# A two-layer vision tower on one core: value moves waited for part by part, attention pairs finished two at a time, and other idle products

## The chip, the core and the metric

The kernel runs on one NeuronCore of a Trainium2 chip, as one launch. The metric is the device time in microseconds, and lower is better. The core has TensorE (matmuls, written to the accumulation memory PSUM), VectorE, ScalarE, GpSimd, and SyncE, whose queue here only starts DMA transfers. Each engine works through its own list of instructions in order and waits on semaphores for the others.

## The reference

The input is 16 images of 3x96x96. They become 36 patches each and a class token, so 37 tokens of width 256 per image and 592 in all, which the kernel holds in five tiles of 128 rows. Then, with residual additions:

```python
h = tokens(x)                                   # patch embedding, class token, positions
h = h + attention0(layernorm(h))                # 16 heads of 16, quantised, ternary weights
h = h + ffn0(layernorm(h))                      # shared expert and the best two of 8 experts
h = h + tower1(layernorm(h))                    # two attention layers (global, local), 4 value heads
w = (weights >= 0.0) * 2.0 - 1.0                # last projection
h = h + clip(layernorm(h) @ w.T * scale + bias, -100, 100)
```

The end of the first attention matters most here:

```python
att = jnp.einsum('bhnr,bhmr->bhnm', ql, kl) / math.sqrt(dk)
y = jax.nn.softmax(att, axis=-1) @ v
y = y.transpose(0, 2, 1, 3).reshape(B, N, d)
return quant4(y) @ ternary_weight(Wo_w).T
```

`quant4` takes the largest absolute value of each token's row, divides by it, multiplies by 7 and rounds.

## The kernel before

Nothing schedules the work. The order on each engine is the order in which the code for that engine is written, and every dependence is a semaphore written by hand. An operation that writes "waits y" runs when the semaphore `y` has reached a count.

**The pair loop of the first tower.** The 16 images are taken as 8 pairs. For a pair, TensorE does `probs_T` (transposes the probabilities of pair p, L1561), `scores` of pair p + 2 (L1549), `values` of pair p (L1574) and four idle products (`spare_products`, L1593); in the last two pairs four wider idle products (`spare`, L1436) stand in the place of the scores. Idle products compute nothing that is read. They give TensorE work between its tasks. `spare` and `spare_products` multiply bf16 data, and `keep_clock` (L1442) multiplies 128x512 fp32 data, which the trace shows as two records each. VectorE does `shift(p)` (row maxima, L895, and their subtraction, L901) and then `finish_y(p - 2)`: the reciprocal of the softmax sums (L911), the product with it (L913), the row maximum for the quantisation (L918), its scaling (L919), its reciprocal (L921) and the rounding (L922). ScalarE does the exponentials (L534), copies the transposed probabilities out of PSUM (L540), and converts the rounded rows (L544, `whole_y`). `values` of pair p writes PSUM bank 6 + p % 2, so it waits until the pair before the last has been read (semaphore `y`):

```python
for p in range(PAIRS + 2):
    if p < PAIRS:
        shift(p)
    if p >= 2:
        finish_y(p - 2)
```

After the loop, TensorE turns the rows (`turn_y`, L1610), spreads the factors of the quantisation over the tokens (L1620, waits `ma7`), does one `keep_clock` product, and then the attention's output product (L1630, waits `yT`).

**The second tower, twice.** `project(t)` computes queries, keys and, from tile 2 on, values of token tile t (L1860). ScalarE copies these values into `v_tok` (L664). The attention needs them per image in `vo`, and since images don't begin at a tile's border, SyncE moves them with small DMAs (L465): 20 per layer, for images 8 to 15, in group 2 (images 8 to 11) and group 3 (12 to 15). TensorE's `values(grp)` (L1931) waits for the moves of its group, `d_v2` or `d_v3`. Images 0 to 7 take another way, without DMAs.

**The last projection.** TensorE writes the bias into the banks of the first four tiles (`bias(t)`, L1972, a product with one row of ones; each waits until VectorE has read that bank, semaphore `bn`), transposes the normalised rows (L1643, waits `xn`), and multiplies in three products per half of the contraction (L1662 to L1664). VectorE clips (L1315), adds (L1316), and SyncE stores.

The functions that the diff touches:

## Time and profile before

| what | value |
|---|---|
| median of 3 runs | 330.63 us (328.04 to 330.92) |
| the profiled execution, its own time | 332.31 us |
| its span, first to last instruction | 330.3 us |
| busy share of the span: TensorE, VectorE, ScalarE, GpSimd | 94%, 66%, 49%, 46% |
| TensorE's mean granted clock | 0.967 of full |

The span leaves out the start and the end of the launch, 2.0 us here. The busy share of TensorE counts idle products too, so 94% says little about how much of it is needed. The chain of waits, followed back from the last instruction, says more.

### The profile page before, as it was taken

The page shows a single profiled execution, that of the slowest core. Times are in us where ns is not written, and L with a number is a line of the kernel's source. Part 1 is how long each engine was busy: PE and PEld are TensorE (multiplying, and loading weights), DVE is VectorE, ACT ScalarE, POOL GpSimd, SP SyncE. Part 2 cuts the span into 40 slices and gives each one's busy share as a digit, 9 for nine tenths or more (in the row PEclk, how much of TensorE's full clock was granted, in tenths as well). Part 3 has the DMA queues.
Part 4 walks back from the last instruction along what each step waited for, and adds up shares of the span by engine and source line. Part 5 has one row for each costly group of instructions (what it writes and reads, how often), then busy time and mean ns, then how long its engine had stood idle before and what let it go on. Part 6 is the DMA issues. An engine that isn't in the chain of part 4 may idle for free.

```text
span 330.3 us, 8349 instructions
## 1 busy us (share of the span) xinstructions
PE 309.3 (94%) x3406; PEld 260.3 (79%) x3408; DVE 217.0 (66%) x574; ACT 160.4 (49%) x353; POOL 153.1 (46%) x178
## 2 busy tenths in 40 slices
PE   7999999999898898999999999999699998999886
PEld 5775678876588888999999999999575676567765
DVE  1089898997877434455655545453577986898674
ACT  0304575556343135576667676763221694169410
POOL 1201209910334782698879888986582000410020
PEclk9999999998979979999999999999979999999987
DMA  7992001320021252537666566514800000000002
GB/s 267 403 396 92 3 0 57 127 99 2 1 96 50 89 167 83 177 127 240 212 221 203 183 217 206 196 34 119 269 4 0 3 9 5 2 1 9 5 2 73
DMA packets 18879, 36.74 MB, mean 111 GB/s; under 512 B 4602, under 2 KB 12849, under 8 KB 18840
## 3 DMA queue, kind: packets, MB, share of 16 engines
q1 hardware_dynamic: 17440, 33.35, 30.2%
q0 software_dynamic: 960, 2.43, 2.3%
q8 instruction: 28, 0.46, 0.5%
q10 hardware_dynamic: 440, 0.41, 0.5%
q14 instruction: 11, 0.09, 0.1%
HBM read 30.28 MB, written 5.75 MB: 109 GB/s over the span
## 4 chain that ended last, share of the span: by engine, by line
PE 60%; DVE 17%; SPq 8%; issue 5%; ACT 5%; DMA 2%; another core or an unknown queue 1%; POOL 1%; ACTq 0%; DVEq 0%; POOLq 0%
PE ps L1662 13%; PE ps L1663 11%; PE ps L1664 11%; SPq L465 8%; PE ps L1442 4%; PE ps L1860 3%; PE ps L1549 2%; PE ps L1454 2%; PE ps L1449 1%; DMA vo<-v_tok 1%; PE ps L1517 1%; PE ps L1561 1%; DVE stats L789 1%; PE ps L1824 1%; PE ps L1574 1%
## 5 line engine op out<-in xcount | busy, mean ns | idle before, releaser
L1339 POOL TENSOR_TENSOR w0l<-raw,w0h 128x384 fp32r<-128x384 f32 (+1 forms) x60 | 56.3, 975 | 15.7 <-ACT w0h L573 15.3
L1089 DVE TENSOR_TENSOR ps<-gact,ps 128x256 f32<-128x256 f32 (+3 forms) x60 | 26.2, 437 | 40.6 <-ACT gact L592 39.0
L1355 POOL TENSOR_TENSOR rstd<-vtmp,cst 128x3 f32<-128x3 f32 (+1 forms) x8 | 6.7, 840 | 91.3 <-DVE vtmp L799 46.3
L1339 POOL TENSOR_TENSOR w1l<-raw,w1h 128x384 fp32r<-128x384 f32 (+1 forms) x48 | 44.8, 971 | 6.5 <-ACT w1h L573 5.7
L592 ACT ACTIVATE gact<-ps 128x256 f32<-128x256 f32 (+3 forms) x60 | 23.2, 387 | 24.8 <-PE ps L1664 16.5
L1094 DVE TENSOR_TENSOR hrl<-ps,hrh 128x256 fp32r<-128x256 f32 (+1 forms) x48 | 20.3, 423 | 18.5 <-ACT hrh L596 17.6
L596 ACT ACTIVATE hrh<-ps 128x256 fp32r<-128x256 f32 (+1 forms) x48 | 18.5, 384 | 27.2 <-DVE ps L1089 26.0
L1662 PE MATMUL ps<-xg0h,w1h 128*128 128x256 f32 x88 | 25.8, 293 | 0.0
L1662 PE MATMUL ps<-xg1h,w0h 128*128 128x256 f32 x88 | 25.6, 291 | 0.0
L1442 PE MATMUL ps<-cst 128*128 128x512 f32 x54 | 25.3, 614 | 0.0
L1663 PE MATMUL ps<-xg1l,w0h 128*128 128x256 f32 x88 | 24.9, 283 | 0.0
L1663 PE MATMUL ps<-xg0l,w1h 128*128 128x256 f32 x88 | 24.9, 283 | 0.0
L1664 PE MATMUL ps<-xg1h,w0l 128*128 128x256 f32 x88 | 24.9, 283 | 0.0
L1664 PE MATMUL ps<-xg0h,w1l 128*128 128x256 f32 x88 | 24.9, 282 | 0.0
L1442 PEld LDWEIGHTS ps<-cst 128*128 128x128 f32 x54 | 10.1, 194 | 10.4 <-issue 10.0
L573 ACT ACTIVATE w0h<-raw 128x768 fp32r<-128x768 f32 (+1 forms) x24 | 18.0, 800 | 0.0
L573 ACT ACTIVATE w1h<-raw 128x768 fp32r<-128x768 f32 (+1 forms) x24 | 17.8, 800 | 0.0
L1662 PEld LDWEIGHTS ps<-xg1h,w0h 128*128 128x128 f32 x88 | 16.8, 191 | 0.5
L1662 PEld LDWEIGHTS ps<-xg0h,w1h 128*128 128x128 f32 x88 | 16.8, 191 | 0.5
L1662 PE MATMUL ps<-w0h,hrh 128*128 128x256 f32 (+1 forms) x48 | 14.0, 293 | 3.3 <-DVE hrl L1094 3.1
L1663 PEld LDWEIGHTS ps<-xg1l,w0h 128*128 128x128 f32 x88 | 16.9, 192 | 0.0
L1664 PEld LDWEIGHTS ps<-xg1h,w0l 128*128 128x128 f32 x88 | 16.9, 191 | 0.0
(309 smaller groups left out, 898.7 us busy)
## 6 DMA issues: line engine op xcount, KB each, us to landing
raw<-in_wexp SPq DMA_DIRECT2D x18, 768.0 KB, 4.3
raw<-in_wexp SPq DMA_DIRECT2D x9, 640.0 KB, 4.4
xg_d<-zero SPq DMA_DIRECT2D x8, 256.0 KB, 10.7
xgs<-xg_d SPq DMA_DIRECT2D x8, 256.0 KB, 4.6
stage_l<-in_xT SPq DMA_DIRECT2D x6, 320.0 KB, 5.0
yg_d<-y SPq DMA_DIRECT2D x7, 256.0 KB
stage_l<-in_tokW SPq DMA_DIRECT2D x6, 128.0 KB, 5.0
stage_l<-in_wq SPq DMA_DIRECT2D x1, 512.0 KB, 5.2
```

Source lines behind the costliest of these rows:

```text
L465: sp.dma_start(vo[n0:n0 + m, b, :, e, :], src[:, :, e, :]).then_inc(S(f"d_v{grp}"), 16)
L573: A(wset[x % 2][0][:, o:o + n], raw[:, o:o + n], ACT.Copy).then_inc(S("w_hi"), 1)
L592: A(gact[i % 2][rows_of(c), 0:n], gate[:, 0:n], ACT.Silu).then_inc(S("silu"), 1)
L596: A(dst[rows_of(c)], product, ACT.Copy).then_inc(S("hh"), 1)
L1089: V.tensor_tensor(up, gact[i % 2][rows_of(c), 0:n], up, ALU.mult).then_inc(S("hm"), 1)
L1094: V.tensor_tensor(dst[r], product, hi[r].bitcast(F32), ALU.subtract).then_inc(S("hl"), 1)
L1339: last = nc.gpsimd.tensor_tensor(wset[i][1][w], raw[w], wset[i][0][w].bitcast(F32), ALU.subtract)
L1442: M(bank(b), ones, cst[:, 0:BK], start=True, stop=True)
L1662: M(dst, a[0], b[0], start=start, stop=False, skip_group_check=skip)
L1663: M(dst, a[0], b[1], start=False, stop=False, skip_group_check=skip)
L1664: return M(dst, a[1], b[0], start=False, stop=stop, skip_group_check=skip)
L1860: last = M(bank(QKB[t % 2])[:, 0:width], xnT[:, k, t * P:(t + 1) * P], w["wq"][:, k, 0:width], start=(k == 0), stop=(k == DC - 1))
```

## The change

It has three parts.

1. SyncE's wait for `v_tok` stands before each piece of an image's rows, and asks only for the tile in which the piece lies. Before, it stood once per group and asked for the last tile of the group. The moves and their order are the same.
2. In the first tower `finish` takes two pairs at a time for pairs 0 to 5, with instructions of twice the size, behind both shifts of the next two pairs. Pairs 6 and 7 are finished singly. `spare_products` has two products instead of four. Behind the pair loop, two bf16 idle products stand ahead of the wait for the factors, and three bf16 ones stand where one `keep_clock` product stood.
3. At the last projection two `keep_clock` products stand between the third bias and the transposes, and three bf16 idle products behind the transposes. The fourth bias comes behind them.

```diff
+        FINISH = [(p, 2) for p in range(0, PAIRS - 2, 2)] + [(PAIRS - 2, 1), (PAIRS - 1, 1)]
...
             for li in range(2):
                 for grp in (2, 3):
-                    sp.wait_ge(S("v_tok"), (TT - MOVED) * li + grp + 2 - MOVED)
-                    if li == 0:
+                    if li == 0 and grp == 2:
                         sp.wait_ge(S("cleared"), 2)
                     for b in range(4 * grp, 4 * grp + 4):
                         for lo, hi in rows_of_batch(b):
+                            sp.wait_ge(S("v_tok"), (TT - MOVED) * li + lo // P + 1 - MOVED)
                             for e in range(2):
...
-            def finish_y(p):
-
-                dve.wait_ge(S("y_mm"), p + 1)
-                yv = bank(6 + p % 2)[:, 0:H * VW].rearrange("p (j w) -> p j w", w=VW)
-                link(V.reciprocal(rz[:, p % 2, :], yv[:, :, DH]))
-                y = yq[:, p, :]
-                V.tensor_tensor(y.rearrange("p (j w) -> p j w", w=DH), yv[:, :, 0:DH],
-                                rz[:, p % 2, :].unsqueeze(2).to_broadcast([P, H, DH]),
-                                ALU.mult).then_inc(S("y"), 1)
-                dve.wait_ge(S("y"), p + 1)
-                m = ma2[:, p:p + 1]
+            def finish(first, n):
+
+                done = FINISH.index((first, n)) + 1
+                pairs = slice(first, first + n)
+                dve.wait_ge(S("y_mm"), first + n)
+                yv = bank(6 + first % 2, n).rearrange("p (a c) -> p a c", a=n)[:, :, 0:H * VW].rearrange(
+                    "p a (j w) -> p a j w", w=VW)
+                z = rz[:, first % 2:first % 2 + n, :]
+                link(V.reciprocal(z, yv[:, :, :, DH]))
+                y = yq[:, pairs, :]
+                V.tensor_tensor(y.rearrange("p a (j w) -> p a j w", w=DH), yv[:, :, :, 0:DH],
+                                z.unsqueeze(3).to_broadcast([P, n, H, DH]), ALU.mult).then_inc(S("y"), 1)
+                dve.wait_ge(S("y"), done)
+                m = ma2[:, pairs]
                 link(V.tensor_reduce(m, y, AX_X, ALU.max, apply_absolute_value=True))
                 V.tensor_scalar(m, m, 1e-6, 1.0 / 7.0, ALU.max, ALU.mult).then_inc(S("ma7"), 1)
-                dve.wait_ge(S("ma7"), p + 1)
-                link(V.reciprocal(rma[:, p:p + 1], m))
-                V.tensor_scalar(y, y, rma[:, p:p + 1], MAGIC, ALU.mult, ALU.add).then_inc(S("yr"), 1)
-
-            for p in range(PAIRS + 2):
-                if p < PAIRS:
-                    shift(p)
-                if p >= 2:
-                    finish_y(p - 2)
+                dve.wait_ge(S("ma7"), done)
+                link(V.reciprocal(rma[:, pairs], m))
+                for p in range(first, first + n):
+                    V.tensor_scalar(yq[:, p, :], yq[:, p, :], rma[:, p:p + 1], MAGIC, ALU.mult,
+                                    ALU.add).then_inc(S("yr"), 1)
+
+            for i in range(PAIRS // 2):
+                shift(2 * i)
+                shift(2 * i + 1)
+                if i >= 1:
+                    finish(2 * i - 2, 2)
+            finish(PAIRS - 2, 1)
+            finish(PAIRS - 1, 1)
...
                 pe.wait_ge(S("pt"), p + 1)
                 if p >= 2:
-                    pe.wait_ge(S("y"), p - 1)
+                    pe.wait_ge(S("y"), p // 2)
...
             def spare_products():
-                for _ in range(4):
+                for _ in range(2):
...
             for p in range(PAIRS - 1):
                 turn_y(p)
-            pe.wait_ge(S("ma7"), PAIRS)
+            spare(2, 5)
+            pe.wait_ge(S("ma7"), len(FINISH))
...
             turn_y(PAIRS - 1)
-            keep_clock(1, 1)
+            spare(3, 5)
...
-            for t in range(4):
+            for t in range(3):
                 pe.wait_ge(S("bn"), TT * 4 + t + 1)
                 bias(t)
+            pe.wait_ge(S("bn"), TT * 4 + 4)
+            keep_clock(2, 3)
             transposes(4)
+            spare(3, 3)
+            bias(3)
```

How the instructions stand in a row, at three places. The line numbers of the changed kernel are a few higher.

SyncE in layer 0, the moves of group 2 (`vo` is where the values go, `v_tok` where they come from). Before:

```order
L465 DMA vo<-v_tok 37x2x16 [waits cleared,v_tok]
L465 DMA vo<-v_tok 37x2x16 x3
L465 DMA vo<-v_tok 14x2x16 x2
L465 DMA vo<-v_tok 23x2x16 x2
L465 DMA vo<-v_tok 37x2x16 x2
```

The same ten moves in the changed kernel:

```order
L466 DMA vo<-v_tok 37x2x16 [waits v_tok,cleared]
L466 DMA vo<-v_tok 37x2x16
L466 DMA vo<-v_tok 37x2x16 [waits v_tok]
L466 DMA vo<-v_tok 37x2x16
L466 DMA vo<-v_tok 14x2x16 [waits v_tok]
L466 DMA vo<-v_tok 14x2x16
L466 DMA vo<-v_tok 23x2x16 [waits v_tok]
L466 DMA vo<-v_tok 23x2x16
L466 DMA vo<-v_tok 37x2x16 [waits v_tok]
L466 DMA vo<-v_tok 37x2x16
```

No move changes its place. The six up to the 14 rows of image 10 lie in tile 2 and wait for its copy alone, and the other four wait for tile 3.

VectorE in the first tower (`mx` are row maxima, `rz` reciprocals of sums, `ma` the factors of the quantisation). Before, from the shift of pair 2 on:

```order
L895 TENSOR_REDUCE mx<-ps 128x8 [waits sc_mm]
L895 TENSOR_REDUCE mx<-ps 128x8
L901 TENSOR_TENSOR stage_l<-ps,mx 128x296 [waits pt_mm,dve_chain]
L901 TENSOR_TENSOR stage_l<-ps,mx 128x296
L911 RECIPROCAL rz<-ps 128x16 [waits y_mm]
L913 TENSOR_TENSOR stage_l<-ps,rz 128x256 [waits dve_chain]
L918 TENSOR_REDUCE ma<-stage_l 128x1 [waits y]
L919 TENSOR_SCALAR ma<-ma 128x1 [waits dve_chain]
L921 RECIPROCAL rma<-ma 128x1 [waits ma7]
L922 TENSOR_SCALAR stage_l<-stage_l,rma 128x256 [waits dve_chain]
```

In the changed kernel, from the shift of pair 3 on:

```order
L896 TENSOR_REDUCE mx<-ps 128x8 [waits sc_mm]
L896 TENSOR_REDUCE mx<-ps 128x8
L902 TENSOR_TENSOR stage_l<-ps,mx 128x296 [waits pt_mm,dve_chain]
L902 TENSOR_TENSOR stage_l<-ps,mx 128x296
L916 RECIPROCAL rz<-ps 128x32 [waits y_mm]
L918 TENSOR_TENSOR stage_l<-ps,rz 128x512 [waits dve_chain]
L922 TENSOR_REDUCE ma<-stage_l 128x2 [waits y]
L923 TENSOR_SCALAR ma<-ma 128x2 [waits dve_chain]
L925 RECIPROCAL rma<-ma 128x2 [waits ma7]
L927 TENSOR_SCALAR stage_l<-stage_l,rma 128x256 [waits dve_chain]
L927 TENSOR_SCALAR stage_l<-stage_l,rma 128x256
```

The finish of pair 0 has moved behind the shift of pair 3 and takes pair 1 with it: seven instructions for two pairs where twelve stood.

TensorE at the last projection (`sml` holds the bias, `cst` constants, `xn` the normalised rows). Before:

```order
L1972 MATMUL ps<-sml,cst 128x256 [waits bn] x4
L1643 MATMUL ps<-cst,xn 128x128 [waits xn]
L1643 MATMUL ps<-cst,xn 128x128
...
L1643 MATMUL ps<-cst,xn 128x128 [waits xn]
L1643 MATMUL ps<-cst,xn 128x128
```

In the changed kernel:

```order
L1981 MATMUL ps<-sml,cst 128x256 [waits bn] x3
L1450 MATMUL ps<-cst 128x512 [waits bn]
L1450 MATMUL ps<-cst 128x512
...
L1652 MATMUL ps<-cst,xn 128x128 [waits xn]
L1652 MATMUL ps<-cst,xn 128x128
L1444 MATMUL ps<-sq,identb 128x512 x3
L1981 MATMUL ps<-sml,cst 128x256
```

Two wide idle products stand ahead of the transposes and three behind them, and the fourth bias is now the last thing before the projection's products.

## Rows read from the trace of the kernel before

**Rows 1.** The page, chain of waits by engine, shares of the span

```profile
PE 60%; DVE 17%; SPq 8%; issue 5%; ACT 5%; DMA 2%; another core or an unknown queue 1%; POOL 1%; ACTq 0%; DVEq 0%; POOLq 0%
```

**Rows 2.** Timeline of VectorE in the pair loop: start us, us, engine, line, operation, idle before

```profile
53.62 0.84 DVE L895 TENSOR_REDUCE mx<-ps 128x8 f32<-128x296 f32 x2 [1.37 <-PE ps L1549]
...
66.73 0.25 DVE L911 RECIPROCAL rz<-ps 128x16 f32<-128x16 f32 x1
67.01 0.42 DVE L913 TENSOR_TENSOR stage_l<-ps,rz 128x256 f32<-128x256 f32 x1
...
68.31 0.35 DVE L922 TENSOR_SCALAR stage_l<-stage_l,rma 128x256 f32<-128x256 f32 x1
68.58 0.83 DVE L895 TENSOR_REDUCE mx<-ps 128x8 f32<-128x296 f32 x2
...
70.20 0.25 DVE L911 RECIPROCAL rz<-ps 128x16 f32<-128x16 f32 x1
```

**Rows 3.** Groups by line, 52 to 80 us: busy us, mean ns, idle before

```profile
L922 DVE TENSOR_SCALAR stage_l<-stage_l,rma 128x256 f32<-128x256 f32 x8 | 3.9, 486 | 0.3
```

**Rows 4.** Timeline of VectorE, rotation in layer 0 of the second tower

```profile
255.58 0.82 DVE L1218 TENSOR_TENSOR stage_l1a<-ps,rot_s 128x640 f32<-128x640 f32 x1 [1.07 <-PE ps L1860]
```

**Rows 5.** Timeline of TensorE, one pair of the pair loop

```profile
54.27 0.61 PE L1593 MATMUL ps<-sq,identb 128*128 128x256 bf16 x4
54.72 0.82 PE L1561 MATMUL ps<-cst,stage_l 128*111 128x128 f32 x6
...
57.50 0.61 PE L1593 MATMUL ps<-sq,identb 128*128 128x256 bf16 x4
```

**Rows 6.** Chain of waits ahead of the attention output: start us, us, what

```profile
78.78 1.28 PE ps L1620 x10
...
80.20 1.82 PE ps L1442 x2
```

**Rows 7.** Stretches: us, busy per engine (x instructions), granted clock, DMA share, GB/s

```profile
80.00:81.00 1.00, 1.00 (x5) 0.44 (x4) 0.83 (x3) 0.82 (x2) 0.00 (x0) 0.53 0.00 0
83.00:84.00 1.00, 1.00 (x9) 1.00 (x8) 0.96 (x3) 1.00 (x2) 0.00 (x0) 0.76 0.00 0
319.00:320.00 1.00, 0.49 (x2) 0.09 (x2) 0.94 (x2) 0.89 (x4) 0.00 (x0) 0.50 0.00 0
```

**Rows 8.** Timeline of ScalarE, values of token tile 2, layers 0 and 1

```profile
259.14 0.22 ACT L664 ACTIVATE v_tok<-ps 128x64 f32<-128x64 f32 x1 [1.16 <-PE ps L1860]
...
292.30 0.23 ACT L664 ACTIVATE v_tok<-ps 128x64 f32<-128x64 f32 x1 [0.70 <-PE ps L1860]
```

**Rows 9.** Timeline of SyncE's queue, the moves of both layers

```profile
261.23 14.47 SPq L465 DMA_DIRECT2D vo<-v_tok  x20
...
294.52 14.13 SPq L465 DMA_DIRECT2D vo<-v_tok  x20
```

**Rows 10.** Timeline of TensorE, first record of the last values product, both layers

```profile
277.26 0.34 PE L1931 MATMUL ps<-stage_l1b,vo 128*32 128x74 f32 x8 [1.44 <-DMA vo<-v_tok]
...
310.17 0.34 PE L1931 MATMUL ps<-stage_l1b,vo 128*32 128x74 f32 x8 [1.05 <-DMA vo<-v_tok]
```

**Rows 11.** Timeline of TensorE: idle products, bias, transposes, last projection

```profile
245.49 7.13 PE L1442 MATMUL ps<-cst 128*128 128x512 f32 x16
...
314.99 1.99 PE L1972 MATMUL ps<-sml,cst 1*128 1x256 f32 x8
317.42 2.07 PE L1643 MATMUL ps<-cst,xn 128*128 128x128 f32 x10 [0.44 <-DVE xn L807]
320.23 0.55 PE L1662 MATMUL ps<-wfh,xTh 128*128 128x256 f32 x1 [0.74 <-DVE xTl L1311]
```

**Rows 12.** Groups by line, 314 to 330 us, the clips of the last projection

```profile
L1315 DVE TENSOR_SCALAR xn<-ps 128x256 f32<-128x256 f32 x5 | 2.1, 424 | 3.1 <-PE ps L1664 3.1
```

**Rows 13.** Chain of waits in the last projection

```profile
321.00 0.21 PE ps L1664
...
326.83 0.12 PE ps L1664
```

## The prediction

> **What bounds the kernel now.** I read the chain of waits first. TensorE holds 60% of it, VectorE 17%, and SyncE's queue 8%, although SyncE computes nothing [rows 1]. That is the sign that instructions which only start transfers stand on the path. Then I took the three places that the change touches, each with the timeline of the engines that meet there, and asked which wait ends last.
>
> In the pair loop of the first tower, VectorE waits once, 1.37 us before pair 2's first reduction at 53.62, and from there has work without a gap until the factors of pair 7 are ready, just before TensorE uses them at 78.78 [rows 2, 6]. One pair costs it a shift (68.58 to 70.20, 1.62) and a finish (66.73 to 68.58, 1.85), so 3.47 us [rows 2]. TensorE needs 3.23 us for a pair (54.27 to 57.50), 0.45 of them idle products (54.27 to 54.72) [rows 5]. So TensorE leads at first and VectorE is the bound by the end.
>
> In the second tower both layers look alike. SyncE starts 20 small moves of values, one after the other, in 14.47 and 14.13 us [rows 9], and TensorE stands still 1.44 and 1.05 us before the last values product, waiting for them to land [rows 10].
>
> At the last projection TensorE had 0.50 of its clock from about 319 on, the 1.2 GHz level [rows 7]. What it had done before that was eight records of one-row bias products, a pause of 0.44 us, ten transposes and a pause of 0.74 us [rows 11]. At that level a product of 128x256 takes 0.21 us, at 2.4 GHz 0.12 [rows 13], so six for a tile take 1.28 against VectorE's 0.88, and VectorE stands idle 3.1 us in all before its five clips [rows 12].
>
> **The pair loop.** A finish is now done for two pairs at once. What does an instruction of twice the size cost? The rotation over 640 elements took 0.82 us and the product over 256 took 0.42 [rows 2, 4], so 384 elements more cost 0.40, and 256 more 0.27. Of the six steps of a finish, the product and the reduction grow by 0.27 each, the small ones by 0.03 together, and a second rounding costs 0.27 (68.31 to 68.58). So 1.85 becomes about 2.70 for two pairs instead of 3.70. That is 1.00 saved three times, 3.0 us; pairs 6 and 7 stay single.
>
> Against it stands the new order. Pair 0 is finished only behind the shift of pair 3, so VectorE waits for the scores of pair 3, one TensorE period behind those of pair 2. With half the idle products that period is 3.23 - 0.23 = 3.00, so pair 3's shift begins at about 56.5 and the wait is some 1.4 us. From there VectorE has five shifts (8.1), three double finishes (8.1), one single (1.85) and the last up to its factors (1.35): 56.5 + 19.4 = 75.9, and I add 0.3 for short waits on TensorE, which now needs as long for two pairs (6.0) as VectorE (5.94). That is 76.2 against 78.73 before, a gain of 2.5.
>
> One correction. The eight roundings took 0.486 on average where an undisturbed one took 0.35 [rows 2, 3], 1.1 us over in all, the early ones, when GpSimd splits weights. The double finish of pairs 0 and 1 still falls into that time with two roundings back to back. I take 0.5 off, between 0 and 1.3: **2.0 us gained**, from 0.9 to 2.6. The Trainium skill, "SBUF — State Buffer", section "SBUF: two separate sides", calls this an exclusive lock: a VectorE operation in a two-port mode and a GpSimd operation shut each other out for the whole instruction. By it both roundings could be held and the term would be 1.2; no row shows two in a row, so my value stays.
>
> Half the idle products save TensorE 0.23 a pair, which is hidden wherever VectorE is the later one; it is in the 3.00 above and is not counted again. The new wait of the values product is for the double finish that frees two banks. For pair 2 this is ready at about 59.2, when TensorE arrives at 59.4; for pair 6 it is late by some 0.2 (in the 0.3). ScalarE's conversion of pair 0 to whole numbers waits behind the same finish and holds the next copy of probabilities, which TensorE needs only behind the scores of the pair after next.
>
> **Ahead of the attention output.** One full-precision idle product took 1.82 us there, on the path, at a granted clock of 0.53 [rows 6, 7], against 0.89 at full clock (sixteen records in 7.13) [rows 11]. Three small ones of 512 columns cost 3 x 0.22 at full clock and 3 x 0.43 = 1.3 at half. So **0.5 us gained**, from 0 (its data are late) to 0.9 (the clock stays up). The two new ones ahead of the factors fit into VectorE's last finish.
>
> **The second tower.** The first six moves read the token tile whose values are ready 1.84 us sooner in layer 0 (259.14 + 0.22 against a start at 261.23) and 2.0 us in layer 1 (292.30 + 0.23 against 294.52) [rows 8, 9]. They fill some 4 us, and the next tile is there by then, so the whole queue starts and ends that much sooner. What is late next? TensorE had nothing between its own work and the last move for 1.44 and 1.05 us [rows 10]; behind those it is bound by itself. VectorE and ScalarE wait for that product. So **2.5 us gained**. Eight more instructions per layer carry a wait. Layer 0, whose two waits are for two semaphores each, took 0.34 longer than layer 1, so a wait costs at most 0.17, eight at most 1.4. The moves have 0.4 and 0.9 to spare, so the gain could fall to 1.0. A wait of one semaphore adds nothing that layer 1 shows, and I take 2.5.
>
> **The last projection.** Two full-precision idle products (four records, 1.77 at full clock [rows 11]) start behind the third bias product at about 316.2 and end at 318.0. The transposes then run back to back and the first three tiles are through 0.1 later than before. Three small products (0.65) and one bias product fall into the former pause of 0.74. If the clock stays at 2.4 GHz, VectorE waits some 0.6 before its first clip and not again: 3.1 - 0.6 = 2.5, less 0.1. That is **2.4 us for the profiled execution**. If the clock falls anyway the gain is 0, and if it has fallen before, the two products take 3.6 and the loss is up to 2.3.
>
> **Sum.** Against the profiled execution (332.31, span 330.3) it is 2.0 + 0.5 + 2.5 + 2.4 = 7.4, giving 324.9. The median of the runs shown is 330.63, 1.68 less. Part of that may be a shorter stretch at half clock at the end, so for the median I count 1.7 for the last term instead of 2.4: 330.63 - 6.7 = **323.9 us**, 2.0% faster.
>
> **Rivals.**
> The clock is not held at the last projection. For it: transposes were the last things before both falls shown [rows 6, 7, 11]. Against it: 1.77 us of dense products are now between. Last term from 0 to +2.3, so 325.6 to 327.9, about 326.2. Chance 15%.
>
> The clock falls once or twice in the pair loop, where only half of the idle products remain. For it: it fell at 80 behind the same kind of small work. Against it: TensorE has no pause there and 0.23 of each 3.00 us is a small share to lose. While it is low TensorE's pair takes up to twice 3.0, so a fall as long as the one from 80 to 83.5 costs 1.7 [rows 7]. Two give 327.3. Chance 12%. The Trainium skill, "TensorE: Matmul & The Clock Gate", section "Part 4: PE-mode transpose", says that transposes don't count as busy for the clock in the way that products do. By it this rival gains weight, and so does the one above; that transposes stand just before the falls at 80 and 319 agrees with it [rows 6, 11].
>
> Instructions of twice the size cost twice the time. Then a double finish saves nothing, the wait for pair 3 stays, and the factors come at 79.7, 1.0 later than before: 323.9 + 3.0 = 326.9. The 640-element row speaks against it [rows 4]. Chance 8%.
>
> The added waits cost 0.17 each, which takes 1.5: 325.4. Chance 5%.
>
> **Slower:** the clock stays low through the whole pair loop. Each pair then costs TensorE up to 6.0 in place of 3.0 and seven pairs lose 21 us: 345. It would need four such pairs to turn 6.7 us of gain into a loss over 1%. The low stretch at 80 ended after 3.5 us of dense work, and that is the ground against it. Chance 4%.
>
> **How the numbers follow.** The forecast holds 56%. The range runs from 321.5 (all upper bounds together give 322.2, and the median is one of three runs that lie 2.9 apart) to 327.5, which takes in the first, third and fourth rival and most of the second. Some 1% is what a measurement of this kernel can tell from no change; the runs shown lie 0.9% apart. Under 327.3 lie the forecast and most of the first four rivals, 84%; between 327.3 and 333.9 the rest of them, 12%; above, 4%.
>
> **What would show it.** In the changed kernel: a VectorE wait of some 1.4 us before pair 3's reduction and the factors of pair 7 ready at about 76.2; a double finish of 2.7; both `vo` queues starting right behind the first `v_tok` copy and under 0.2 us of TensorE idle before the last values product; a granted clock of 1.00 in the last ten us and 0.6 us of VectorE idle before its clips. The prediction is wrong if the clock column drops between 52 and 76, if the double finish takes over 3.3, or if the clips still wait for 3 us.

## The result, and the profile after

Over 20 executions each, on one chip, the kernel before took 333.84 us in the median (328.04 to 336.85) and the changed kernel 327.50 (323.89 to 333.28). The ratio is **0.989, 95% interval 0.985 to 0.994**: 1.1% faster, 3.6 us. It compares only the executions within 1.5% of the fastest of the same kernel, 5 of the 20 before and 14 of the 20 after, so it is not the quotient of the medians, which lie 6.3 us apart. The forecast was 6.7 us, 2.0%. The profiled execution took 326.40 us (span 324.4) against 332.31 (330.3), 5.9 less. Its first 1.0 us is no part of the change: pair 2's first reduction begins at 52.60 instead of 53.62 [rows 2], and nothing ahead of it was touched.

The page of the changed kernel, its chain of waits by engine, answers to [rows 1]:

```profile
span 324.4 us, 8319 instructions
...
PE 65%; DVE 20%; ACT 5%; issue 4%; another core or an unknown queue 2%; DMA 1%; POOL 1%; ACTq 0%; DVEq 0%; POOLq 0%
```

SyncE's queue (8% before) has left the chain, and VectorE has 20% of it instead of 17%.

I cut every execution into the same five stages. **A**, pair loop: from pair 2's first reduction to TensorE's product with the factors. **B**: from there to the first addition to `h`. **C**: from layer 0's first rotation on VectorE to layer 1's. **D**: from that to the first bias of the last projection. **E**: from that bias to the last addition. Each is the difference of two start times in the timelines. Before: 25.16, 4.13, 33.08, 26.33, 12.81. After: 24.11, 3.45, 31.97, 25.69, 10.98. That is 1.05 + 0.68 + 1.11 + 0.64 + 1.83 = 5.3 us. What lies between B and C, the experts, is not changed and gave 0.4 back (172.67 to 173.09).

**The pair loop.** Timeline of VectorE in the changed kernel, the first double finish from pair 3's reduction on, the scaling of the second, the end of the third and the two single ones (start, us, what, idle before):

```profile
55.62 0.84 DVE L896 TENSOR_REDUCE mx<-ps 128x8 f32<-128x296 f32 x2 [1.31 <-PE ps L1557]
...
57.25 0.35 DVE L916 RECIPROCAL rz<-ps 128x32 f32<-128x32 f32 x1
57.63 0.69 DVE L918 TENSOR_TENSOR stage_l<-ps,rz 128x512 f32<-128x512 f32 x1
58.35 0.69 DVE L922 TENSOR_REDUCE ma<-stage_l 128x2 f32<-128x512 f32 x1
59.08 0.49 DVE L923 TENSOR_SCALAR ma<-ma 128x2 f32<-128x2 f32 x1
...
59.80 0.86 DVE L927 TENSOR_SCALAR stage_l<-stage_l,rma 128x256 f32<-128x256 f32 x2
60.59 0.82 DVE L896 TENSOR_REDUCE mx<-ps 128x8 f32<-128x296 f32 x2
...
65.65 0.60 DVE L923 TENSOR_SCALAR ma<-ma 128x2 f32<-128x2 f32 x1
...
72.12 0.17 DVE L923 TENSOR_SCALAR ma<-ma 128x2 f32<-128x2 f32 x1
...
73.05 0.25 DVE L916 RECIPROCAL rz<-ps 128x16 f32<-128x16 f32 x1
...
75.30 0.26 DVE L916 RECIPROCAL rz<-ps 128x16 f32<-128x16 f32 x1 [0.31 <-PE ps L1582]
```

GpSimd in the same stretch (its groups hold several instructions each):

```profile
59.04 2.00 POOL L1381 CAST w0h<-raw 128x384 fp32r<-128x384 f32 x4
...
64.94 1.29 POOL L1386 TENSOR_TENSOR wo0l<-wo0q,wo0h 128x512 fp32r<-128x512 f32 x1
```

VectorE waits 1.31 us for pair 3's scores, as forecast (1.4). The double finish without disturbance, the third, takes 70.29 to 73.05, 2.76 us, as forecast (2.70). The first took 3.34 (57.25 to 60.59) and the second 3.20. Look at the scaling, two elements per partition: 0.17 us in the third, 0.49 and 0.60 in the others. The first began at 59.08, just behind the start of a GpSimd cast at 59.04 (four in 2.00 us, so about 0.5 each), and ended with it. The second began at 65.65 while GpSimd's subtraction of 64.94 ran, and ended at 66.25 where that ended, at 66.23. The clock stayed at 1.00.

**The second tower.** TensorE in layer 0, the end of the values product of group 2 (`values(2)`), the output product behind it, and the last values product; then the one interrupted record of layer 1:

```profile
271.99 0.65 PE L1940 MATMUL ps<-stage_l1b,vo 128*32 128x74 f32 x7
272.40 0.31 PE L1940 MATMUL ps<-stage_l1b,zo 128*32 128x74 f32 x3
272.48 0.23 PE L1940 MATMUL ps<-stage_l1b,vo 128*32 128x74 f32 x1
272.49 0.35 PE L1940 MATMUL ps<-stage_l1b,zo 128*32 128x74 f32 x5
272.77 1.13 PE L1950 MATMUL ps<-wo_g,ozp 128*128 128x256 f32 x4
273.83 0.34 PE L1940 MATMUL ps<-stage_l1b,vo 128*32 128x74 f32 x8
```

```profile
304.17 0.22 PE L1940 MATMUL ps<-stage_l1b,vo 128*32 128x74 f32 x1 [0.20 <-issue]
```

The idle 1.44 and 1.05 us before the last values product [rows 10] are gone. But the product ahead of it, whose 64 multiplications took 1.16 us before (273.54 to 274.70), now took 1.57 (271.20 to 272.77) and in layer 1 1.64. Nothing it waits for is late: the one idle time that the trace names there is "issue", TensorE without instructions.

**The last projection.** TensorE, then VectorE:

```profile
310.91 1.56 PE L1981 MATMUL ps<-sml,cst 1*128 1x256 f32 x6
312.39 1.98 PE L1450 MATMUL ps<-cst 128*128 128x512 f32 x4
314.22 1.25 PE L1652 MATMUL ps<-cst,xn 128*128 128x128 f32 x10
...
316.76 0.35 PE L1671 MATMUL ps<-wfh,xTh 128*128 128x256 f32 x1
```

```profile
315.59 1.68 DVE L1319 TENSOR_TENSOR xTl<-ps,xTh 128x384 fp32r<-128x384 f32 x4 [0.85 <-ACT xTh L737]
317.75 0.42 DVE L1323 TENSOR_SCALAR xn<-ps 128x256 f32<-128x256 f32 x1 [0.47 <-PE ps L1673]
...
321.43 0.42 DVE L1323 TENSOR_SCALAR xn<-ps 128x256 f32<-128x256 f32 x1 [0.42 <-PE ps L1673]
```

```profile
317.00:322.00 5.00, 4.39 (x32) 3.72 (x31) 3.94 (x11) 0.00 (x0) 0.00 (x0) 1.00 0.25 85
```

The granted clock is 1.00 until the last addition is through, and six products for a tile take 0.79 us or less (clips begin at 317.75, 318.55, 319.34). VectorE waits 0.85 + 0.47 + 0.42 = 1.7 us from the last normalised rows on: before the subtraction that needs the transposed rows, before the first clip, and before the last. In the kernel before it was 0.24 for the transposed rows and 3.1 at the clips [rows 12].

### The profile page after: what moved, and what is told of

It is laid out like the page before. It is cut to its first block, busy times and chain, and to the rows that moved or that the text cites. A ratio compares the mean times of both kernels' runs of the same rounds, so it can differ in the third digit from the quotient of the medians.

```text
span 324.4 us, 8319 instructions
## 1 busy us (share of the span) xinstructions
PE 305.1 (94%) x3398; PEld 255.8 (79%) x3402; DVE 216.0 (67%) x559; ACT 160.2 (49%) x353; POOL 153.2 (47%) x178
## 4 chain that ended last, share of the span: by engine, by line
PE 65%; DVE 20%; ACT 5%; issue 4%; another core or an unknown queue 2%; DMA 1%; POOL 1%; ACTq 0%; DVEq 0%; POOLq 0%
PE ps L1671 12%; PE ps L1673 11%; PE ps L1672 10%; PE ps L1869 4%; PE ps L1940 3%; PE ps L1912 3%; PE ps L1557 2%; PE ps L1462 2%; PE ps L1950 2%; PE ps L1450 2%; DVE ps L1097 2%; PE ps L1457 1%; PE ps L1894 1%; PE ps L1569 1%
```

## The experiments

All numbers are of stages as cut above. "Ratio" is against the kernel before on the same chip.

```
kernel                        A      B      C      D      E     ratio (95%)
before                      25.16   4.13  33.08  26.33  12.81   1
changed                     24.11   3.45  31.97  25.69  10.98   0.989 (0.985 to 0.994)
e1_moves                    25.24   3.46  31.81  25.21  12.74   0.998 (0.993 to 1.003)
e2_pairs                    23.91   3.45  33.04  26.32  13.01   0.995 (0.991 to 0.999)
e3_last                     25.14   3.93  33.04  26.32  10.99   0.989 (0.983 to 0.995)
e4_idle_only                27.14   3.46  33.03  26.33  11.64   1.003 (0.998 to 1.007)
e5_pad                      25.17   3.45  31.81  25.20  10.99   0.981 (0.975 to 0.987)
e6_other_form               24.62   3.46  31.98  25.68  10.92   0.985 (0.979 to 0.990)
e7_late_split               23.00   3.45  32.25  25.72  10.99   1.015 (1.010 to 1.020)
e8_one_idle                 27.33   3.46  32.95  25.41  10.70   0.985 (0.980 to 0.989)
e9_short_pool               24.13   3.46  33.31  25.40  10.98   0.982 (0.973 to 0.991)
e10_four_idle               24.41   3.45  31.64  25.63  10.99   0.987 (0.982 to 0.992)
e11_late_weights            24.12   3.45  31.98  25.99  10.99   0.994 (0.989 to 0.999)
e12_together                24.78   3.45  31.72  25.21  10.69   0.987 (0.982 to 0.993)
e13_changed_again           24.10   3.45  32.95  25.41  10.99   0.990 (0.985 to 0.995)
e14_parts_1_and_3           25.22   3.45  31.58  25.21  10.98   0.985 (0.979 to 0.991)
```

A stage is good to some 0.1 us where nothing disturbs it, a ratio to no better than 0.5%. Stages come from one profile of each run. The causes below rest on stages and rows; ratios are only used for the whole. Between B and C lie the experts, which the three parts don't touch and which took 167.1 to 174.1 us (187.8 in e7); that spread is larger than the gain, and it is in every total.

### One part at a time

**e1_moves**: the kernel before with part 1 alone.

```diff
-                    sp.wait_ge(S("v_tok"), (TT - MOVED) * li + grp + 2 - MOVED)
...
+                            sp.wait_ge(S("v_tok"), (TT - MOVED) * li + lo // P + 1 - MOVED)
```

> The kernel before with part 1 alone (a wait ahead of each piece of the value moves). In the changed kernel the idle time of 1.44 and 1.05 us before the last values products is gone, but the values product of group 2 took 1.57 and 1.64 us instead of 1.16, so only 1.10 and 0.65 us came out. Theory 1: these 0.4 us in each layer are pauses in which TensorE waits for its own instructions, and they depend on where in its program the products lie. TensorE's list is here that of the kernel before, so the pauses are absent, the gain is 2.3 to 2.5 us, ratio 0.993. Theory 2: the 0.4 us come from the moves being earlier (their packets or their semaphore events meet the products of group 2). Then they are here too and the gain is 1.75 us, ratio 0.995. In both, no idle time over 0.2 us before the last values products.

Theory 1 holds for the gain: C and D are 1.27 and 1.12 us shorter, 2.4 in all. The values product of group 2 took 1.41 us in layer 0 (271.13 to 272.54) and 1.17 in layer 1, so a pause of 0.25 us is left in layer 0 where none was expected. In e3_last, with the moves as before, it took 1.44 there. The output product that follows and the last values product stand back to back with it.

```profile
271.13 0.34 PE L1931 MATMUL ps<-stage_l1b,vo 128*32 128x74 f32 x8
...
272.30 0.31 PE L1931 MATMUL ps<-stage_l1b,zo 128*32 128x74 f32 x8
272.54 1.13 PE L1941 MATMUL ps<-wo_g,ozp 128*128 128x256 f32 x4
273.60 0.34 PE L1931 MATMUL ps<-stage_l1b,vo 128*32 128x74 f32 x8
```

So part 1 by itself gives what was forecast, and the pauses of 0.4 us and more are not of its making. The ratio, 0.998, doesn't show it: its interval reaches from 0.993.

**e2_pairs**: the kernel before with part 2 alone, its diff as in the change above (`finish`, `spare_products`, and the idle products behind the loop).

> The kernel before with part 2 alone (first tower: two pairs finished at a time, half the idle products, small ones behind the loop). By the trace of the changed kernel: from pair 2's first reduction to TensorE's use of the factors 24.1 us instead of 25.2, from there to the first addition to h 3.45 instead of 4.13, together 1.7 us and a ratio of 0.995. Theory 1 (what VectorE does is the bound, and it is held by GpSimd as before): 24.1 here too, double finishes of 3.3, 3.2 and 2.8 us. Rival: the gain is given back behind the attention, where the clock falls at some other place (granted clock under 0.9 between 78 and 94 us for longer than in the kernel before): ratio 0.998 to 1.002. If the pauses in the second tower hang on where TensorE's program lies, the values products of group 2 take 1.6 us here as in the changed kernel, although the moves are as before.

The loop gains 1.25 us, and the pauses in the values product are here, with the moves as they were: TensorE pauses for some 0.4 us in it, and the idle time before the last values product shrinks by about as much, from 1.44 and 1.05 to 0.98 and 0.55. C and D stay as before.

```profile
272.23 0.66 PE L1940 MATMUL ps<-stage_l1b,vo 128*32 128x74 f32 x7
...
273.02 1.13 PE L1950 MATMUL ps<-wo_g,ozp 128*128 128x256 f32 x4
275.13 0.34 PE L1940 MATMUL ps<-stage_l1b,vo 128*32 128x74 f32 x8 [0.98 <-DMA vo<-v_tok]
```

In the kernel with part 2 alone the pause costs nothing, because it is taken out of a wait. Part 1 removes that wait, and the pause comes to light. The ratio, 0.995, is the one expected for a gain of 1.7 us; its interval leaves room for the rival's 0.998 too. Of these 1.7, 0.68 lie in stage B, and e1 has the same B (3.46) with the old code.

**e3_last**: the kernel before with part 3 alone.

```diff
-            for t in range(4):
+            for t in range(3):
...
+            pe.wait_ge(S("bn"), TT * 4 + 4)
+            keep_clock(2, 3)
             transposes(4)
+            spare(3, 3)
+            bias(3)
```

> The kernel before with part 3 alone (idle products at the last projection). By the trace of the changed kernel, from the first bias to the end of the span 13.5 us instead of 15.3, so 1.8 us and a ratio of 0.9945; VectorE idle some 1.7 us in all from the last normalised rows to its last clip (3.3 before). Rival: in the repeats of the kernel before the clock is often up at this place by itself, and the idle products only delay the transposes there by 0.8 us: a ratio of 0.997 to 1.001 although the profile shows the clock held.

E is 10.99 against 12.81: 1.8 us, and the clock at 1.00. The rival's 0.997 to 1.001 lies outside the interval. The ratio (0.989) is lower than this stage explains (0.9945); its profile began 4 us earlier than the others (pair 2's first reduction at 48.83), which has nothing to do with the edit. The kernel before doesn't always lose the same here: e1 12.74, e2 13.01, and e4, with the same code at this place, 11.64, because the low stretch began at 320.2 there and was half as long.

**e4_idle_only**: the kernel before with the idle products of part 2 alone, pairs finished one by one.

```diff
             def spare_products():
-                for _ in range(4):
+                for _ in range(2):
...
-            keep_clock(1, 1)
+            spare(3, 5)
```

> The kernel before with the idle products of part 2 alone: two instead of four per pair, two and three small ones behind the loop in place of the full-precision one. Pairs are finished one by one as before. Theory 1 (VectorE sets the end of the pair loop, 3.47 us a pair): the factors are used 25.0 to 25.2 us after pair 2's first reduction, as before, and 0.7 us are gained from there to the first addition to h, ratio 0.998. Rival (TensorE sets it): 0.23 a pair less, factors 1 us earlier, ratio 0.995, and finishing two pairs at once would have brought nothing.

Neither theory: the loop took 27.14, 2.0 us more than before. TensorE stood 1.62 us at 68.9 without instructions, and from 71.0 to 74.4 its granted clock was 0.50. That was the rival I had given 12%, with a pause ahead of the fall that I had not foreseen. Because of it this run doesn't tell the two theories apart.

### Where TensorE's instructions lie

**e5_pad**: the changed kernel with 13 small idle products more in a wait of TensorE.

```diff
             keep_clock(3, 0)
+            for _ in range(13):
+                M(bank(0)[:, 0:8], identb[:, :], sq0[:, 0, 0:8], start=True, stop=True)
             transposes(1)
```

> The changed kernel with 13 more idle products of 8 columns on TensorE, ahead of the first transposes behind the attention, where TensorE waits 1.3 us for VectorE anyway. They bring TensorE's list in the second tower back to where it stood in the kernel before, since part 2 took 13 more products out than it put in. Theory 1 (the 0.4 us pauses in the values product of group 2 hang on where TensorE's instructions lie): that product takes 1.16 us again instead of 1.57 and 1.64, the second tower gives 2.4 us instead of 1.75, and the whole is 0.6 us under the changed kernel. Theory 2 (the pauses come from the moves being earlier, or from anything else of the change): 1.6 us as in the changed kernel. The pad itself costs at most 13 x 0.02 us beside the wait.

Theory 1. C and D are 31.81 and 25.20, those of e1 to 0.01 us, 0.65 better than the changed kernel, and the values product of group 2 took 1.41 and 1.16 us as in e1, not 1.16 in both layers. The same stages in the seven profiles with the changed kernel's list of TensorE at this place (changed, e6, e7, e8, e9, e11, e13) add up to between 57.66 and 58.71, 58.10 on average; in the four with the list of before (e1, e5, e12, e14) to between 56.79 and 57.02. With the moves as before it was 59.41. So **the place of the list decides over about half of what part 1 gives**, 1.3 or 2.5 us on average. The same list doesn't give the same pauses each time: in e13, the changed kernel once more, the values products of groups 1 and 2 of layer 0 took 1.55 and 2.15 us, and C was 32.95, hardly less than before. What makes the difference between two executions stays open. Its loop took 25.17, with a fall of the clock from 66.4 to 69.8.

**e11_late_weights**: the changed kernel with the third weight transfer of the pair loop held back.

```diff
             for part in range(3):
+                if part == 2:
+                    sp.wait_ge(S("y_mm"), PAIRS - 1)
                 next_load(1, part)
```

> The changed kernel with the third weight transfer of the pair loop (768 KB, started at about 65 us) held back until the values of pair 6 are through, at about 73 us. In two profiles TensorE's next block of 16 KB of instructions began to land at 68.3 instead of 66.2 while that transfer ran, TensorE stood 1.6 and 1.9 us and the clock fell behind it. Theory 1 (the block waits behind the transfer): it lands from about 66.2 in under 1.0 us instead of 1.3 to 1.6, no pause of TensorE at 69 us (0.25 in the changed kernel), no fall in the loop, 23.9 us for it. Theory 2 (the pauses have another source): 0.2 us or more at the same instruction. ScalarE needs these weights only behind the attention, so nothing should be lost there.

This run is best read beside e8_one_idle (below), the changed kernel up to its last projection, whose loop took 27.33. Timeline of TensorE in e8, and the clock behind it:

```profile
68.55 0.29 PE L1582 MATMUL ps<-stage_l 111*37 111x51 f32 x4
70.73 1.15 PE L1582 MATMUL ps<-stage_l 111*37 111x51 f32 x20 [1.89 <-issue]
```

```profile
66.00:70.70 4.70, 2.84 (x89) 2.39 (x84) 4.09 (x12) 2.42 (x4) 0.02 (x1) 1.00 0.45 156
70.80:74.20 3.40, 3.40 (x30) 2.70 (x30) 2.10 (x6) 0.46 (x1) 0.00 (x0) 0.50 0.02 5
```

The queues in e8 from 66 to 68.3, and then from 68.3 to 70.6 (queue, kind: packets, MB, share of 16 engines; "instruction" brings the engines' instructions in blocks of 16 KB):

```profile
q1 hardware_dynamic: 118, 0.70, 86.2%
```

```profile
q8 instruction: 1, 0.02, 2.7%
```

The same 66 to 68.3 in the changed kernel and in e11:

```profile
q1 hardware_dynamic: 106, 0.65, 84.9%
q8 instruction: 1, 0.02, 4.2%
```

```profile
q8 instruction: 1, 0.02, 2.9%
```

In e8 the block of instructions came only when the weights (86% of the DMA engines) were through, and TensorE stood 1.89 us. In the changed kernel it got in between and TensorE stood 0.25. With the weights out of the way, in e11, it took 1.08 us instead of 1.56, there was no pause at this instruction, and no fall. Theory 1 for this instruction, but the loop stayed at 24.12 instead of the 23.9 expected. VectorE's wait before pair 7's finish did shrink, from 0.31 to 0.11 us. But TensorE paused 0.30 us at another place, among the scores at 65.59, and VectorE's shift behind them came 0.2 later, at 69.34. (e2, with neither pause, took 23.91.) The ratio of e11, 0.994, shows no gain either. That the long pause of e4 and e8 is the wait behind the weights is read from the order of their packets; of the eight profiles with two idle products per pair and the transfer in its place (all such but e7 and e11) six had no long pause, so one profile without it doesn't show that the edit prevents it. In e4 and e8 the fall stands right behind the pause. In e5 it came without one, 2.3 us behind a wait of 0.41 us for ScalarE that the changed kernel has too (0.39), without a fall. What decides there stays open.

### VectorE and GpSimd

**e6_other_form**: the changed kernel with the rounding and the scaling in the three-operand form.

```diff
-                V.tensor_scalar(m, m, 1e-6, 1.0 / 7.0, ALU.max, ALU.mult).then_inc(S("ma7"), 1)
+                V.scalar_tensor_tensor(m, m, 1e-6, seventh[:, 0:n], ALU.max, ALU.mult).then_inc(S("ma7"), 1)
...
-                    V.tensor_scalar(yq[:, p, :], yq[:, p, :], rma[:, p:p + 1], MAGIC, ALU.mult,
-                                    ALU.add).then_inc(S("yr"), 1)
+                    V.scalar_tensor_tensor(yq[:, p, :], yq[:, p, :], rma[:, p:p + 1],
+                                           cst[:, C_UNM:C_UNM + 1].to_broadcast([P, D]), ALU.mult,
+                                           ALU.subtract).then_inc(S("yr"), 1)
```

> The changed kernel with the rounding and the scaling of the row maxima written in VectorE's three-operand form (scalar_tensor_tensor, the constant read from a tile) instead of tensor_scalar. Theory 1: the tensor_scalar form is held while a GpSimd instruction runs (the scaling took 0.49 and 0.60 us instead of 0.17, and ended with GpSimd's cast and subtraction), and the three-operand form, like the product with the reciprocals (0.69 us in all three double finishes), isn't. Then the scaling takes some 0.2 us everywhere, the rounding about 0.45 everywhere instead of 0.31 undisturbed, the three double finishes cost about 3.0 each instead of 3.34, 3.20 and 2.76, and the loop is within 0.4 us of the changed kernel. Theory 2: the holding hits any VectorE instruction that reads and writes SBUF only: 0.5 to 0.6 for the scaling and over 0.8 for the first two roundings again, and the loop is 0.8 us longer.

```profile
59.45 0.52 DVE L925 SCALAR_TENSOR_TENSOR ma<-ma,seventh 128x2 f32<-128x2 f32 x1
...
66.31 0.59 DVE L925 SCALAR_TENSOR_TENSOR ma<-ma,seventh 128x2 f32<-128x2 f32 x1
...
73.00 0.16 DVE L925 SCALAR_TENSOR_TENSOR ma<-ma,seventh 128x2 f32<-128x2 f32 x1
```

Theory 2 on what is held: 0.52 and 0.59 against 0.16 undisturbed. The form doesn't help, and the rounding costs 0.13 more each time; the loop is 0.5 us longer, not 0.8. As a rule for every instruction between SBUF and SBUF theory 2 is too wide: the reduction ahead of the scaling took 0.69 in all three double finishes, although in the changed kernel the one of 64.92 ran beside GpSimd's subtraction of 64.94. The Trainium skill, "SBUF — State Buffer", section "SBUF: two separate sides", counts a VectorE instruction with two inputs in SBUF among those that contend with a reading GpSimd instruction; by that rule this form had to be held, and the trace agrees. The product with the reciprocals, one of whose inputs lies in PSUM, took 0.69 in all three double finishes.

**e7_late_split**: the changed kernel with GpSimd's weight split behind the loop.

```diff
+                    pool.wait_ge(S("ma7"), len(FINISH))
                     for part in range(3):
                         pool.wait_ge(S(f"d_raw{part}"), 16)
```

> The changed kernel with GpSimd's casts and subtractions for the weights of the first expert (11.6 us of work) put behind the factors of the last pair; the subtraction for the attention's output weights, 1.3 us, stands ahead of them. GpSimd is idle in the pair loop, and the weight transfers that wait for its buffers come later too. Theory 1 (VectorE was held by GpSimd for about 1.0 us in all): all three double finishes take 2.76 us, and the factors are used 23.1 us after pair 2's first reduction instead of 24.1. Rival (TensorE's periods and its instruction pauses are as near a bound as VectorE): double finishes of 2.76 us but the loop not under 23.8, with VectorE waiting for TensorE instead. Behind the loop some of the gain, or more, can be lost at the first expert, whose weights are late.

```profile
58.90 0.17 DVE L923 TENSOR_SCALAR ma<-ma 128x2 f32<-128x2 f32 x1
...
59.30 0.61 DVE L927 TENSOR_SCALAR stage_l<-stage_l,rma 128x256 f32<-128x256 f32 x2
59.83 0.83 DVE L896 TENSOR_REDUCE mx<-ps 128x8 f32<-128x296 f32 x2
```

Theory 1, to 0.1 us: all three double finishes take 2.76, the loop 23.00. So GpSimd costs the changed loop 1.1 us, not 0.5. (The weight transfers left the loop with it, but 1.0 of the 1.1 is in the two finishes, 3.34 + 3.20 - 2 x 2.76.) The kernel as a whole is 1.5% slower: the reciprocal roots of the layer norm are GpSimd's too and stand behind the split, so the first normalised rows came 14.0 us behind the first addition to `h` instead of 5.3.

**e9_short_pool**: the changed kernel with the split in pieces of half the size (and the subtraction for `wo0l` in four).

```diff
-                        n = WPART[part] // 4
+                        n = WPART[part] // 8
```

> The changed kernel with GpSimd's casts and subtractions for the first expert in pieces of half the size (8 instead of 4 per part, about 0.24 and 0.48 us each), and the one for the attention's output weights in four pieces (0.33 each) instead of one of 1.29. Theory 1: a held VectorE instruction runs when the GpSimd instruction of the moment ends (in the changed kernel the scaling of the first double finish ended at 59.57 and GpSimd's first cast of that part began at 59.04 and lasted about 0.5). With pieces of half the length the holds are half as long: 1.0 us over in all becomes 0.5, the first two double finishes 3.0 each, the loop 23.6 us. Theory 2: VectorE and GpSimd take turns and lose the same share of time whatever the size: 1.0 over in all, and the loop stays at 24.1 or more.

```profile
58.66 0.32 DVE L923 TENSOR_SCALAR ma<-ma 128x2 f32<-128x2 f32 x1
...
59.22 0.90 DVE L927 TENSOR_SCALAR stage_l<-stage_l,rma 128x256 f32<-128x256 f32 x2
...
65.11 0.55 DVE L923 TENSOR_SCALAR ma<-ma 128x2 f32<-128x2 f32 x1
...
65.89 1.04 DVE L927 TENSOR_SCALAR stage_l<-stage_l,rma 128x256 f32<-128x256 f32 x2
```

Theory 2. The first scaling is held for less (0.32 instead of 0.49), but the roundings behind it for more: 0.90 and 1.04 for two instead of 0.62. Over in all, 0.15 + 0.28 + 0.38 + 0.42 = 1.2 us; the loop 24.13.

### The last projection, and the whole

**e8_one_idle**: the changed kernel with one full-precision idle product less.

```diff
-            keep_clock(2, 3)
+            keep_clock(1, 3)
             transposes(4)
```

> The changed kernel with one full-precision idle product instead of two ahead of the last transposes. In the changed kernel the transposes began 1.5 us after the first normalised rows could be read, behind 1.98 us of idle products, and the stretch from the first bias to the last clip was 10.5 us. Theory 1: one such product (0.99 us) is enough for the clock, and the transposes begin 0.85 us sooner: 9.7 to 9.9 us, 0.7 us gained. Theory 2: the clock falls as in the kernel before: granted clock 0.50 in most of the last ten us, and the stretch is 12.3 us or more.

One product is enough, the clock stays at 1.00. But only 0.28 us came of it (E 10.70), not 0.7: the transposes began sooner and then waited for the normalised rows, 1.88 us instead of 1.25 for ten. In the changed kernel they had been late by 0.9, not by the 1.5 of the expectation.

**e10_four_idle**: the changed kernel with four idle products per pair.

```diff
             def spare_products():
-                for _ in range(2):
+                for _ in range(4):
```

> The changed kernel with four idle products per pair as before, two pairs finished at a time. In three profiles with four the clock never fell between 52 and 79 us and TensorE never stood for over 0.5 us without instructions; in four of the seven with two it did one or the other, or both, and the pair loop took 25.2 to 27.3 us instead of 24.1. Theory 1 (half the idle products are what lets the clock fall): no fall here, the loop 24.3 to 24.6 us because TensorE's period is 3.23 and VectorE waits a little longer at pair 3, and the second tower without the 0.4 us pauses, since TensorE's list is again within three products of the kernel before. Theory 2 (it is the chance meeting of TensorE's instruction blocks with the weight transfers): a pause or a fall can show here too.

The loop took 24.41 as theory 1 has it. The pauses in the second tower are smaller but not gone as it has it: the values product of group 2 took 1.23 and 1.52 us, and C + D is 57.27, between the two groups of e5. (The count ahead of this run was off: a fall or a pause of over 0.5 us stood in three of the seven profiles with two, e4, e5 and e8, not in four.) In six profiles with four idle products (before, e1, e3, e10, e12, e14) no long pause and no fall stands in the loop; in ten with two (changed, e2, e4 to e9, e11, e13) there are two long pauses and three falls. If four or two made no difference, all three profiles with a fall would still be among those ten about one time in five, so that four of them prevent it is not shown.

**e12_together**: the edits of e8, e10 and e11, and the list of TensorE in its old place:

```diff
-            spare(2, 5)
             pe.wait_ge(S("ma7"), len(FINISH))
...
-            spare(3, 5)
+            spare(2, 5)
```

> The changed kernel with what the runs so far point to: four idle products per pair (no fall in the pair loop in four profiles with four), the third weight transfer held back to about 73 us, one full-precision idle product at the last projection instead of two, and behind the pair loop two small idle products in all, which puts TensorE's list in the second tower exactly where it stood before. Expected from the stages seen: pair loop 24.4 us (25.16 before), 3.45 to the first addition (4.13), second tower 2.4 gained as with part 1 alone, last stretch 2.1 to 2.2 gained. Together some 6 us, 1.8%, under the kernel before, and 0.3 to 1 us under the changed kernel. If the executions with a long pause in the pair loop are what the changed kernel loses in the median, then 1 to 1.5 us under it.

C, D and E are as expected, 4.6 us under the kernel before. The loop took 24.78 instead of 24.4: TensorE paused 0.30 us at 65.26 and VectorE then waited 0.60 at 69.43. The stages add up to 5.7 us; the ratio is 0.987, where 0.982 was expected.

**e13_changed_again**, the changed kernel without any edit, and **e14_parts_1_and_3**, the diffs of e1 and e3 together, ran on the same chip as e12:

> The changed kernel itself, beside the two other runs on one chip. If its median gain over the kernel before is what one profile shows less the start of the kernel (4.9 us of 332), the ratio is 0.985. If in every third execution or so the pair loop takes 27.3 us instead of 24.1, as in one of the two profiles of variants whose TensorE list is the same up to there, the ratio is 0.988 to 0.990. Its profile: double finishes of 3.2 to 3.4 us twice and then 2.76; the pair loop 24.1 or, with a pause of over 1.5 us or a fall, 25.2 to 27.3.

> The kernel before with parts 1 and 3 and without part 2 (the first tower as before). Its own stages: pair loop 25.1 to 25.2 us, second tower 2.4 us gained, without pauses in the values product of group 2, last stretch 1.8 gained. Together 4.2 us, ratio 0.987. Theory 1 (part 2 earns 1.05 in the loop in good executions, loses 0.65 in the second tower through the place of TensorE's list, and 1 to 3 us in executions where the clock falls in the loop): this kernel is as fast in the median as the whole change or faster, by up to 0.5%. Rival (part 2 gives 1.7 us as in its own profile): it is 1.1 us slower than the whole change.

The changed kernel gave 0.990 again (median 323.90), without part 2 it was 0.985 (321.66), e12 0.987 (321.29). The intervals overlap, so I don't call these two faster. By the rival e14 had to be 1.1 us slower than e13, and it came out faster, which speaks for theory 1; six executions against twelve are too few to rule the rival out. The stages of e14 are as expected. The values product of group 2 took 1.16 us in both layers. The profiled execution took 325.31 us all the same, because the experts took 171.8 in it, against 168.0 in e12 and 167.7 in e13.

## Why the prediction was off

**What went right.** The sign, the three places and their mechanisms. VectorE's wait for pair 3 (1.31 for 1.4), the double finish (2.76 for 2.70), the queue of moves starting 3.88 us behind the layer's first rotation instead of 5.65 (257.13 and 253.25, before 261.23 and 255.58), 1.8 us sooner for a forecast of 1.84, no idle time before the last values product, part 1 by itself (2.4 for 2.5), the clock held at the last projection, which the rival with 15% denied. The Trainium skill, "TensorE: Matmul & The Clock Gate", section "Part 4: PE-mode transpose", has it that transposes count less as busy. If they do, it decided nothing here: ten of them, between one or two full-precision products and three small ones, did not bring the clock down before the last addition in any of twelve profiles (changed, e3, e5 to e14). One of the forecast's own signs of being wrong did come in the profile, a double finish of over 3.3 us: the first took 3.34.

**Which steps failed.** In the order of the sum:

1. *"The double finish of pairs 0 and 1 still falls into that time [...]. I take 0.5 off."* The mis-sized term. GpSimd costs 1.1 us in the changed loop, as much as in the loop before (e7, and the rows at 59.08 and 65.65). I had looked only at the rounding, the one instruction that was long in the trace of before, and at one of the double finishes. In the changed order the scaling of two of them met GpSimd and lost 0.32 and 0.43, and the two roundings of the first lost 0.24. Another 0.1 came from pair 3's reduction, which began 3.02 behind pair 2's (by the forecast's own period of 3.00 it had to be 56.6, not 56.5), 0.2 from the three double finishes and 0.1 from VectorE's second wait (0.31 before pair 7's finish). So 2.0 became 1.05. The forecast's other value, 1.2 by the Trainium skill's "SBUF — State Buffer", section "SBUF: two separate sides", was nearer in size, by luck: it was worked out for the two roundings, and what was held most were the scalings.
2. *"While it is low TensorE's pair takes up to twice 3.0 [...]. Two give 327.3. Chance 12%."* The fall in the loop happened in three of ten profiles, in two of them behind a pause of 1.6 and 1.9 us in which, by the order of the packets, TensorE's instructions waited behind a weight transfer. I had written that TensorE has no pause there. Over the five profiles with the changed loop's code and nothing else moved in it (changed, e2, e5, e8, e13) the loop took 24.92 on average, so the term is worth about **0.3 us, not 2.0**.
3. *"What is late next? TensorE had nothing between its own work and the last move [...]; behind those it is bound by itself."* True, and it had a pause of its own there. With part 2's shorter list the values products of groups 1 and 2 lost 0.2 to 1.7 us in a layer to pauses (least and most in e9: 1.37 instead of 1.16, and 1.90 + 2.15 instead of 2.32). The term is worth **1.3 us on average, not 2.5**. The added waits cost nothing (e1).
4. *"That is 2.4 us for the profiled execution", 1.7 for the median.* It measured 1.8, and 1.6 against the average of the four profiles with the old code (12.81, 12.74, 13.01, 11.64). The two idle products ran 1.98 us (312.39 on), so the transposes began some 0.9 us behind the first normalised rows and VectorE waited 0.85 before its subtraction (0.24 before the change), where I had put the tiles 0.1 later. The 0.42 before the last clip, where I had put none, came on top; some 0.3 came back, since a clip and its addition take 0.80 us back to back and not the 0.88 that I had read. The value for the median held.
5. *"0.5 us gained"* ahead of the attention output: 0.68 in the pair of profiles, but e1 and e14 show 3.46 and 3.45 with the old code. It is a matter of whether the clock happens to be low there: the four profiles with the old code (before, e1, e3, e14) average 3.74, so the term is worth some 0.3.

Summed, 0.3 + 0.3 + 1.3 + 1.6 = 3.5 us, and the ratio gives 3.6. That it fits is partly luck, since these are means over four to seven profiles, and those of the loop lie 3.4 us apart. The medians of all twenty lie 6.3 us apart, near the forecast's 6.7; no run settles which of the two is the gain of a typical execution, and that nearness would be luck as well, since the terms above were not what was forecast. The range, 321.5 to 327.5, ended where the median came out, mainly because the median of the three executions shown (330.63) was 3.2 us under that of twenty (333.84).

## What to carry to other kernels

When a wait on the path goes, look for what was hidden in it, a pause for instructions too, and judge an edit that removes instructions by what the shift does to tight stretches further on. Before counting on a faster engine, list every instruction of it that another engine can hold, not only those that were held in the trace at hand. And an effect that a single profile shows at a place where the clock sometimes falls is worth its average over executions: take more than one profile before believing a term of a microsecond or two.

## What the runs showed of the hardware

- Blocks of 16 KB of instructions come over the DMA engines during the kernel, in about 1 us each when the engines are free (2.7% of 16 engines' 2.3 us in e8) and in 1.56 us beside a weight transfer (the changed kernel). In e8 one came only behind a 768 KB weight transfer; TensorE stood 1.89 us without instructions, and the clock was 0.50 for the next 3.4.
- Thirteen idle products of 8 columns, some 170 us ahead of the second tower, took 0.65 us out of its two layers (e5). What they changed there is only where in TensorE's list its products lie; that the pauses come at the ends of instruction blocks is inferred.
- A VectorE instruction on two elements per partition took 0.17 us alone and up to 0.60 beside GpSimd, in both forms tried, and until the GpSimd instruction ended. Cutting GpSimd's instructions in half didn't lessen the sum (e9, 1.2 us over in all against 1.0).
